# Attention with a gated state: work moved off VectorE, and the order of roots, sigmoid and projections

## The chip, the cores and the metric

The kernel runs on one core of a Trainium2 chip. It is one program in one launch. The time is the device time in microseconds of that core. A core has TensorE (PE, matrix products into PSUM), VectorE (DVE), ScalarE (ACT), GpSimd (POOL), and SyncE (SP), whose queue issues the transfers here. The engines run side by side, each through its own list of instructions in order, and meet only at semaphores.

## The reference, cut to what matters

The program computes four layers over 4096 tokens of width 256 (4 sequences of 1024): gated linear attention, a mixture of experts, a memory layer with one gradient step, and a ternary MLP, each followed by a layer norm. Only the first layer and its norm matter here:

```
q, k, v = x @ Wq.T, x @ Wk.T, x @ Wv.T            # 16 heads of 16
q, k = elu(q / 4) + 1, elu(k) + 1
gate = sigmoid(x @ Wg.T + bg)                     # one number per head and token
for t in range(1024):
    S = gate[t] * S + outer(k[t], v[t])           # 16 x 16 per head
    y[t] = q[t] @ S
x = layernorm(x + y @ Wo.T)
```

## The kernel before, in words

`build_attention` cuts each sequence into chunks of 128 tokens. A tile is one chunk of one sequence: 32 tiles j, with T = j // 4 the chunk and b = j % 4 the sequence, so that a block of four tiles shares the chunk. The last four tiles carry no state on (KEPT = 28).

Within a tile the recurrence becomes matrix products. DVE makes the decay matrix of all 16 heads by one scan over 2048 columns (`decay`, L515, tile a_dcy) from gates that SP has spread over 128 partitions (a_gbc). `weigh` (L524) multiplies the scores (L311) by it into a_A, in two instructions. `attend` (L323, L330) sums what the state gives (St times qE) and what the tile's own tokens give (A times v). Sums of decays (ET, L504, one scan for four tiles) are spread over heads by a matmul (`decays`, L271); `decayed_q` (L541) makes qE from it, and L544 copies the decay over the whole tile to a_dec. The state is renewed by `update`: PE multiplies k and v (L343, 16 records per tile); DVE masks the product to the heads' own blocks (a_um, L556) and adds the old state times a_dec, in two instructions (L560). In the first four tiles a masked copy does (L554). `residual` (L568) adds x to the output projection (L285), and bn_stats and bn_aggr (L572, L576) take its mean and variance. POOL computes the inverse root from these for four tiles at once (`spread`, three Newton steps in four operations each), ACT normalises (L450), PE turns the result (`turn_x`, L294), ACT keeps it (L441), PE scores it for the experts (`router`, L300) and ACT copies the scores (L445).

q and k are projected by `project` (L237), one of four quarters of a chunk in each turn. ACT makes elu from it in three activations (L406, L407, L409), POOL adds them into a_qk (`phi`, L610). The gates are projected once per chunk (L246); ACT takes their sigmoid (L416), whose table has to be loaded, and loads the table of exp again (L417). SP writes the gates out (L182) and reads them back spread (`gates_in`, L189), two tiles ahead.

The order is written out by hand: each engine runs a loop over n from FIRST to LAST - 1, and turn n does on each engine the steps of its tiles: scores of n + 1, output of n - 1, attend of n, projection of quarter n + 5, values and transposed k of n + 1, and the later steps of tiles n - 5 to n - 7. DVE in turn n: weigh n, update n - 1, weigh_k n (L532, a_kw), scan n + 1, decayed_q n + 1, residual n - 1, and, each fourth turn, the scan of ET.

Of the kernel before, what the change touches and what calls it, by code (L numbers as in the profile page):

```python
# [17 lines left out]
P = 128  # L18
# [54 lines left out]
def build_attention(nc, io, mem):  # L73

    X, XT, ident = mem["X"], mem["XT"], mem["ident"]
    with ExitStack() as c2:
# [35 lines left out]
        stat = sb("stat", [P, 6])  # L112
        mv = mem["mv"]
        nmean = sb("nmean", [P, B])
# [19 lines left out]
        y_ready, yt_done, u_ready, um_done, st_done = (sem(k) for k in ("y_ready", "yt_done", "u_ready", "um_done", "st_done"))  # L134
# [3 lines left out]
        n_done = sem("n_done")  # L138
        id_done = sem("id_done")
        FIRST, LAST, SP_OPS = -5, NT + 3, 15  # L140
# [13 lines left out]
        def state_read(e, j):  # L154

            if j < 4:
                e.wait_ge(st_done, 2 * (j + 1))
            else:
                e.wait_ge(um_done, j - 3)

        with nc.Block() as block:
            @block.sync
            def _(sp):
# [12 lines left out]
                sp.dma_start(blk[:, :, :], io["blk"]).then_inc(cst_in, 16)  # L176
                sp.dma_start(Wv[:, :, :], io["WvT"].rearrange("(g p) n -> p g n", p=P)).then_inc(wv_in, 16)
# [46 lines left out]
            def _(pe):  # L224
# [25 lines left out]
                def values(j):  # L250
# [5 lines left out]
                    if j >= 8:  # L256
                        pe.wait_ge(xnt_read, j - 7)
# [30 lines left out]
                def turn_x(j):  # L288
                    pe.wait_ge(xn_done, j + 1)
                    pe.wait_ge(v_read, 3 * min(j + 7, NT))  # L290
# [24 lines left out]
                def attend(j):  # L315

                    b = j % 4
                    if j >= 4:
                        pe.wait_ge(qe_done, j - 3)
                        pe.wait_ge(st_done, 2 * (j - 3))  # L320
# [13 lines left out]
                def update(j):  # L334
# [5 lines left out]
                    for g in range(G):  # L340
                        for r in range(4):
                            c = g * P + 32 * r
                            mm = pe.matmul(bK[32 * r:32 * r + 32, 32 * g:32 * g + 32], kw[j % 2][:, c:c + 32], vp[j % 2][:, c:c + 32],  # L343
                                           start=True, stop=True)
                    mm.then_inc(u_ready, 1)

                def turn_k(j):
                    T, b = divmod(j, 4)
                    pe.wait_ge(phi_done, 4 * (T + 1))
                    if j == 0:  # L350
                        pe.wait_ge(cst_in, 64)
# [11 lines left out]
                for n in range(FIRST, LAST):  # L363
# [5 lines left out]
                    if tile(n - 1):  # L369
                        project_out(n - 1)  # L370

                    if n >= -4:
                        if tile(n - 1):
                            pe.wait_ge(yt_done, n)
                        if 1 <= (n + 4) // 4 <= NC and n % 4 == 0:
                            pe.wait_ge(sig_done, (n + 4) // 4)
                        if carries(n - 8):
                            pe.wait_ge(r_read, n - 7)
                    if Q % 4 == 0 and Q < NT:
                        gates(Q // 4)  # L380
                    if carries(n - 7):
                        router(n - 7)
# [3 lines left out]
                    if Q < NT:  # L386
# [3 lines left out]
                    if carries(n - 6):  # L390
                        turn_x(n - 6)
# [6 lines left out]
            def _(act):  # L398
# [20 lines left out]
                def values(j):  # L419
                    act.wait_ge(v_ready, j + 1)  # L420
                    if tile(j - 7):
                        act.wait_ge(xnt_ready, j - 6)
# [15 lines left out]

                def keep_x(j):
# [3 lines left out]
                def score(j):  # L443
                    act.wait_ge(r_ready, j + 1)
                    act.activation(mem["score"][:, j, :], bY[:, R0:R0 + E8], ACT.Copy).then_inc(r_read, 1)  # L445

# [16 lines left out]
                for n in range(FIRST, LAST):  # L463
                    Q = n + 5
                    if n == -2:
                        act.wait_ge(cst_in, 64)
                    if tile(n + 2):
                        masked_q(n + 2)

                    if tile(n):  # L470
                        act.wait_ge(y_ready, n + 1)
                    elif carries(n - 7):
                        act.wait_ge(r_ready, n - 6)
                    if Q % 4 == 0 and Q < NT:
                        gates(Q // 4)
                    if carries(n - 7):
                        score(n - 7)
                    if tile(n):
                        y_out(n)
                    if Q < NT:  # L480
# [3 lines left out]
                    if carries(n - 6):  # L484
                        keep_x(n - 6)
                    if carries(n - 5):
                        normalize(n - 5)

            @block.vector
            def _(v):  # L490
# [8 lines left out]
                def gate_decay(T):  # L499
# [6 lines left out]
                    v.memset(gT[T % 2][:, 0:1], 0.0).then_inc(gz_done, 1)  # L506

# [27 lines left out]
                def decayed_q(j):  # L535
# [7 lines left out]
                    v.wait_ge(st_done, 2 * min(j - 1, KEPT))  # L543
                    v.tensor_copy(dec[j % 2][:, :], bK[:, HALF + P - 1:HALF + D:P]).then_inc(dec_done, 1)  # L544

                def update(j):
# [4 lines left out]
                    if j >= 1:  # L551
                        v.wait_ge(st_done, 2 * j)
                    if j < 4:
# [1620 lines left out]
```

## Time and profile before

| | us |
|---|---|
| three timed runs | 1461.71, 1460.06, 1454.76; median 1460.06 |
| the profiled execution | 1467.62 |
| its span | 1465.6 |
| attention, from the start to the barrier behind it | about 326 |
| one block of four tiles in its middle | 38.52 |

The span is one profiled execution. The attention stage fills its first 326 us; the stages behind it are the same instructions in both kernels, but for one of POOL. Busy time is a sum over instructions of one engine; neighbouring instructions overlap slightly, so that distances between starts are safer than durations. In a list of groups the columns are: line, engine, operation, output and inputs with their shapes, count, then busy us and mean ns of one, then the idle time before them and who ended it. In a timeline the columns are: start, us, engine, line, operation, shapes, count, and in brackets the idle time before it with its releaser.

### The profile page before, as it was taken

What the parts mean: (1) busy time and instruction counts of PE and PEld (TensorE: products, weight loads), DVE (VectorE), ACT (ScalarE), POOL (GpSimd) and SP (SyncE); (2) the same over time, 40 slices, a digit from 0 to 9 for tenths busy, and PEclk for the clock granted to TensorE, in tenths of its full rate; (3) what the DMA queues carried; (4) which work ended last, traced back from release to release, by engine and by line L of the source; (5) the groups of instructions that cost most, each with busy time, mean ns of one, the idle gap of its engine ahead of it and who ended that gap; (6) DMA issues with size and microseconds to landing.
All of it is one profiled execution on the core that took longest, in us unless ns stands there. A gap on an engine that the chain in (4) does not pass through costs nothing. (4 is left out here: it accounts for less than half of the span.)

```text
span 1465.6 us, 21869 instructions
## 1 busy us (share of the span) xinstructions
PE 1345.6 (92%) x7418; PEld 859.6 (59%) x7419; DVE 828.9 (57%) x1676; ACT 536.7 (37%) x1104; POOL 305.6 (21%) x357
## 2 busy tenths in 40 slices
PE   7888888889989899999999997869999999899996
PEld 4556656655545566666666664436665564477774
DVE  5999999986533222222222221457778755676774
ACT  5445554432011122222222221134444532457675
POOL 2133333321653000000000001613220000144444
PEclk9899999999999999999999999989999999999999
DMA  5544544629221011111111112303110000000001
GB/s 192 177 171 172 177 170 158 207 80 370 84 79 61 22 51 43 43 47 46 43 43 50 43 43 90 87 21 105 30 29 1 1 1 11 1 1 15 29 15 58
DMA packets 68226, 112.39 MB, mean 77 GB/s; under 512 B 9008, under 2 KB 53936, under 8 KB 64048
## 3 DMA queue, kind: packets, MB, share of 16 engines
q1 hardware_dynamic: 61584, 94.49, 19.2%
q0 software_dynamic: 6144, 16.79, 3.6%
q8 instruction: 50, 0.82, 0.2%
q14 instruction: 32, 0.26, 0.1%
q10 hardware_dynamic: 416, 0.03, 0.0%
HBM read 79.70 MB, written 31.59 MB: 76 GB/s over the span
## 5 line engine op out<-in xcount | busy, mean ns | idle before, releaser
L1684 POOL DMA_INDIRECT m_got<-outs,slot x64 | 61.2, 957 | 562.7 <-DMA outs<-XT 448.1
L1089 DVE TENSOR_TENSOR ro_h<-ro_bB,ro_sl 128x512 f32<-128x512 f32 x71 | 49.1, 692 | 218.5 <-PE ro_bB L1038 218.5
L515 DVE TENSOR_TENSOR_SCAN a_dcy<-a_gbc,a_ident 128x2048 f32<-128x2048 f32 x32 | 144.6, 4520 | 11.2 <-DMA a_gbc<-gd 7.3
L2040 POOL TENSOR_TENSOR q_hr<-q_hf,q_hr 128x512 fp32r<-128x512 f32 x64 | 83.9, 1322 | 287.0 <-ACT q_hr L1881 287.0
L1033 PE MATMUL ro_bA<-Win,ro_xT 128*128 x284 | 135.9, 601 | 0.7 <-ACT ro_xT L1060 0.6
L1045 PE MATMUL ro_bO<-Wout,ro_hT 128*128 x568 | 134.3, 379 | 0.9 <-DVE ro_hT L1082 0.9
L1045 PEld LDWEIGHTS ro_bO<-Wout,ro_hT 128*128 128x128 f32 x568 | 107.8, 190 | 45.6 <-issue 34.6
L1038 PE MATMUL ro_bB<-Wsw,ro_xT 128*128 x284 | 133.5, 592 | 0.0
L1082 DVE COPY ro_hT<-ro_bH 128x512 f32<-128x512 f32 x71 | 49.1, 691 | 101.2 <-PE ro_bH L1018 101.2
L1069 ACT ACTIVATE XT<-ro_bO 128x256 f32<-128x256 f32 x71 | 27.2, 383 | 204.9 <-PE ro_bO L1045 204.9
L1038 PEld LDWEIGHTS ro_bB<-Wsw,ro_xT 128*128 128x128 f32 x284 | 54.0, 190 | 68.2 <-issue 68.2
L1806 PE MATMUL q_bO<-W2r,q_hr 128*128 128x256 f32 x512 | 75.9, 294 | 6.8 <-POOL q_hr L2040 6.7
L610 POOL TENSOR_TENSOR a_qk<-a_eb,a_rb 128x512 f32<-128x512 f32 x32 | 40.6, 1269 | 182.7 <-ACT a_eb L409 182.2
L1064 ACT ACTIVATE ro_sl<-ro_bA 128x512 f32<-128x512 f32 x71 | 42.4, 597 | 97.3 <-PE ro_bA L1033 97.3
L1806 PEld LDWEIGHTS q_bO<-W2r,q_hr 128*128 128x128 f32 x512 | 66.1, 188 | 19.9 <-POOL q_hr L2040 14.2
L934 POOL DMA_INDIRECT rows<-r_row,r_rix x64 | 63.9, 999 | 65.5 <-DVE r_rix L835 47.9
L311 PE MATMUL a_bS<-a_qm,a_qk 32*128 32x256 f32 x512 | 39.3, 422 | 40.1 <-DVE a_A L524 28.4
L524 DVE TENSOR_TENSOR a_A<-a_bS,a_dcy 128x1024 f32<-128x1024 f32 x64 | 75.3, 1219 | 0.1
L1796 PE MATMUL q_bH<-q_xr,W1r 128*128 128x512 f32 x256 | 70.6, 404 | 3.6 <-ACT q_hr L1881 3.6
L1114 PE MATMUL m_ring<-m_h,m_W 128*128 128x512 f32 x128 | 60.0, 613 | 12.4 <-ACT m_alr L1405 8.9
L1033 PEld LDWEIGHTS ro_bA<-Win,ro_xT 128*128 128x128 f32 x284 | 48.8, 192 | 36.0 <-issue 35.7
L786 ACT ACTIVATE sh_sl<-sh_bA 128x512 f32<-128x512 f32 x28 | 16.6, 597 | 120.2 <-PE sh_bA L724 74.9
(271 smaller groups left out, 2524.1 us busy)
## 6 DMA issues: line engine op xcount, KB each, us to landing
a_gbc<-gd SPq DMA_DIRECT2D x32, 1024.0 KB, 4.8
rows<-a_zero SPq DMA_DIRECT2D x8, 1152.0 KB, 10.5
XT<-rows SPq DMA_DIRECT2D x71, 128.0 KB, 2.0
outs<-XT SPq DMA_DIRECT2D x71, 128.0 KB, 1.7
a_xt<-in_xTt SPq DMA_DIRECT2D x8, 512.0 KB, 3.7
X<-in_x SPq DMA_DIRECT2D x8, 512.0 KB, 5.8
Win<-in_w_in SPq DMA_DIRECT2D x8, 512.0 KB, 10.7
Wsw<-in_w_sw SPq DMA_DIRECT2D x8, 512.0 KB, 10.6
```

Source lines behind the costliest of these rows:

```text
L515: v.tensor_tensor_scan(dcy[:, :], gbc[j % 2][:, :], ident16[:, :], 0.0, ALU.mult, ALU.add).then_inc(d_done, 1)
L524: v.tensor_tensor(A[j % 2][:, 2 * h:2 * h + 2, :, :, :].rearrange("p r g e t -> p r g (e t)"), bS[:, 2 * h:2 * h + 2, :].rearrange("p r (g ...
L934: pool.indirect_dma_start(out=mem["rows"], out_offset=bass.IndirectOffsetOnAxis(ap=rix[p][k][:, 0:1], axis=0), in_=row[p][k][:, :], in_off ...
L1033: mm = pe.matmul(bA[:, :], xT[p][:, g, :], w, start=(g == 0), stop=(g == G - 1))
L1038: mm = pe.matmul(bB[:, :], xT[p][:, g, :], w, start=(g == 0), stop=(g == G - 1))
L1045: mm = pe.matmul(bO[:, 0:D], hT[:, j * P:(j + 1) * P], Wout[:, bass.ds(e, 1), j, :].rearrange("p o f -> p (o f)"), start=(j == 0), stop=(j ...
L1082: v.tensor_copy(hT[:, :], bH[:, :]).then_inc(ht_read, 1)
L1114: mm = pe.matmul(banks[o][:, :], W[:, i, col + o * P:col + (o + 1) * P], rhs(i), start=(i == 0), stop=(i == G - 1))
L1684: pool.indirect_dma_start(out=got[q % 2][k][:, t, :], out_offset=None, in_=mem["outs"], in_offset=bass.IndirectOffsetOnAxis(ap=slot[:, k, ...
L1796: mm = pe.matmul(bH[f % 2][:, :], W1r[:, g, f * P:(f + 1) * P], xr[q % 2][:, part, g, :], start=(g == 0 and part == 0), stop=(g == G - 1 a ...
L1806: mm = pe.matmul(bO[k // 2][:, (k % 2) * D:(k % 2 + 1) * D], hr[:, part, f % 4, k * P:(k + 1) * P], W2r[:, f, :], start=(f == 0 and part = ...
L2040: pool.tensor_tensor(hr[:, 1, f % 4, :], hf[f % 2][:, :], hr[:, 0, f % 4, :], ALU.subtract).then_inc(hl_done, 1)
```

## The change

- State: the DVE additions of L560 go. ACT makes from a_dec a 32 x 32 diagonal matrix per row group and half (`decay_matrix`, two activations of 32 columns), PE adds that matrix times the old state to the same PSUM columns as the product of k and v (16 more records), and DVE does one masked copy for every tile.
- Norm: bn_stats and bn_aggr go from DVE. ACT sums x and its squares about the mean in two activations with an accumulator (`moments`). POOL's root takes one operation less.
- The first four additions of q and k move from POOL to DVE.
- Order: `project` comes before router and attend on PE, and before y_out on ACT, in three turns of four. ACT takes the sigmoid of the gates at the end of the turn, behind project and values, instead of ahead of y_out. DVE takes the scan of ET right behind `weigh` of the next turn. Normalising, turning and scoring come two turns later, and so the loops are two turns longer (LAST = NT + 5).

```diff
-        um = sb("um", [P, G, 32])
+        eye32, dg = sb("eye32", [P, 32]), [sb(f"dg{p}", [P, G, 32]) for p in range(2)]
-        FIRST, LAST, SP_OPS = -5, NT + 3, 15
+        FIRST, LAST, SP_OPS = -5, NT + 5, 14
...
                 # PE, update(j)
-                                           start=True, stop=True)
+                                           start=(g == 0), stop=(j < 4), skip_group_check=True)
+                    if j >= 4:
+                        pe.wait_ge(dg_done, 2 * (j - 3))
+                        pe.wait_ge(st_done, j - 3)
+                        for g in range(G):
+                            for r in range(4):
+                                mm = pe.matmul(bK[32 * r:32 * r + 32, 32 * g:32 * g + 32], dg[j % 2][32 * r:32 * r + 32, g, :],
+                                               St[32 * r:32 * r + 32, j % 4, g, :], start=False, stop=True, skip_group_check=True)
...
                 # PE, the loop
                     if tile(n - 1):
                         project_out(n - 1)
+                    if Q < NT and Q % 4 > 0:
+                        project(Q)
                     if n >= -4:
                         if tile(n - 1):
                             pe.wait_ge(yt_done, n)
-                        if 1 <= (n + 4) // 4 <= NC and n % 4 == 0:
-                            pe.wait_ge(sig_done, (n + 4) // 4)
+                        if n % 4 == 0:
+                            pe.wait_ge(sig_done, min((n + 4) // 4 + 1, NC))
...
-                    if Q < NT:
+                    if Q < NT and Q % 4 == 0:
                         project(Q)
-                    if carries(n - 6):
-                        turn_x(n - 6)
+                    if carries(n - 8):
+                        turn_x(n - 8)
...
                 # ACT
+                def decay_matrix(j):
+                    act.wait_ge(dec_done, j - 3)
+                    if j >= 6:
+                        act.wait_ge(u_ready, j - 1)
+                    for g in range(G):
+                        act.activation(dg[j % 2][:, g, :], eye32[:, :], ACT.Copy, scale=dec[j % 2][:, g:g + 1]).then_inc(dg_done, 1)
+                def moments(j):
...
+                    act.activation(scrap[:, :], X[:, j, :], ACT.Copy, scale=-1.0 / D, accum_out=mv[T % 2][:, b, 0:1]).then_inc(bn_done, 1)
+                    act.wait_ge(bn_done, j + 1)
+                    act.activation(scrap[:, :], X[:, j, :], ACT.Square, bias=mv[T % 2][:, b, 0:1], accum_out=mv[T % 2][:, b, 1:2]).then_inc(ag_done, 1)
...
-                    if Q % 4 == 0 and Q < NT:
-                        gates(Q // 4)
...
                     if tile(n + 1):
                         values(n + 1)
+                    if 0 < Q < NT and Q % 4 == 0:
+                        gates(Q // 4)
+                    if carries(n - 8):
+                        keep_x(n - 8)
+                    if tile(n - 2):
+                        moments(n - 2)
+                    if carries(n - 7):
+                        normalize(n - 7)
...
                 # DVE, update(j)
-                    v.tensor_tensor(um[:, :, :], bK[:, 0:64].rearrange("p (g c) -> p g c", g=G), blk[:, :, :], ALU.mult).then_inc(um_done, 1)
-                    for g in range(G):
-                        v.scalar_tensor_tensor(out=St[:, b, g, :], in0=St[:, b, g, :], scalar=dec[j % 2][:, g:g + 1], in1=um[:, g, :],
-                                               op0=ALU.mult, op1=ALU.add).then_inc(st_done, 1)
+                    v.tensor_tensor(St[:, b, :, :], bK[:, 0:64].rearrange("p (g c) -> p g c", g=G), blk[:, :, :], ALU.mult).then_inc(st_done, 1)
...
                 # DVE, residual(j) and the loop
-                    v.bn_stats(stat[:, :], X[:, j, :]).then_inc(bn_done, 1)
-                    v.bn_aggr(mv[T % 2][:, b, :], stat[:, :]).then_inc(ag_done, 1)
                     if tile(n):
                         weigh(n)
+                    if n >= 0 and n % 4 == 0 and n // 4 + 1 < NC:
+                        gate_decay(n // 4 + 1)
                     if carries(n - 1):
                         update(n - 1)
...
-                    if Q % 4 == 0 and Q < NT:
-                        gate_decay(Q // 4)
+                    if n == FIRST:
+                        gate_decay(0)
+                    if Q < 4:
+                        phi(Q)
```

## Rows read from the trace of the kernel before

**Rows 1.** Busy time by stretches: from:to, us, then each engine (x count), clock, DMA.

```profile
150.00:200.00 50.00, 43.13 (x553) 30.29 (x554) 48.57 (x68) 25.60 (x69) 21.67 (x38) 1.00 0.49 168
```

**Rows 2.** The groups of DVE in the first 330 us.

```profile
L560 DVE SCALAR_TENSOR_TENSOR a_St<-a_St,a_dec,a_um 128x32 f32<-128x32 f32 x48 | 16.9, 392 | 0.8
L572 DVE BATCH_NORM_STATS2 a_stat<-X 128x6 f32<-128x256 f32 x32 | 13.7, 427 | 1.1
...
L576 DVE BATCH_NORM_AGGREGATE mv<-a_stat 128x2 f32<-128x6 f32 x32 | 5.8, 182 | 1.1
```

**Rows 3.** The timeline of DVE over one turn of the middle.

```profile
148.22 2.35 DVE L524 TENSOR_TENSOR a_A<-a_bS,a_dcy 128x1024 f32<-128x1024 f32 x2
150.50 0.21 DVE L556 TENSOR_TENSOR a_um<-a_bK,a_blk 128x64 f32<-128x64 f32 x1
150.75 0.41 DVE L560 SCALAR_TENSOR_TENSOR a_St<-a_St,a_dec,a_um 128x32 f32<-128x32 f32 x2
151.08 0.42 DVE L532 TENSOR_TENSOR a_kw<-a_bK,a_dcy 128x256 f32<-128x256 f32 x1
151.63 4.43 DVE L515 TENSOR_TENSOR_SCAN a_dcy<-a_gbc,a_ident 128x2048 f32<-128x2048 f32 x1
155.97 0.40 DVE L541 TENSOR_TENSOR a_qE<-a_bK,a_qk 128x256 f32<-128x256 f32 x1
...
156.35 0.42 DVE L568 TENSOR_TENSOR X<-a_bK,X 128x256 f32<-128x256 f32 x1
...
157.37 2.35 DVE L524 TENSOR_TENSOR a_A<-a_bS,a_dcy 128x1024 f32<-128x1024 f32 x2
...
159.89 1.07 DVE L560 SCALAR_TENSOR_TENSOR a_St<-a_St,a_dec,a_um 128x32 f32<-128x32 f32 x2
```

**Rows 4.** The timeline of DVE in the first four tiles.

```profile
53.68 0.21 DVE L554 TENSOR_TENSOR a_St<-a_bK,a_blk 128x64 f32<-128x64 f32 x1
53.81 0.41 DVE L532 TENSOR_TENSOR a_kw<-a_bK,a_dcy 128x256 f32<-128x256 f32 x1
```

**Rows 5.** The timeline of PE over a block of four tiles.

```profile
131.31 1.15 PE L311 MATMUL a_bS<-a_qm,a_qk 32*128 32x256 f32 x16 [1.33 <-POOL a_qk L610]
...
136.61 1.98 PE L237 MATMUL a_bQ<-a_xt,a_Wqk 128*128 128x512 f32 x4
...
139.87 0.44 PE L357 MATMUL a_bK<-ident,a_qk 128*128 128x128 f32 x2
...
150.72 1.15 PE L311 MATMUL a_bS<-a_qm,a_qk 32*128 32x256 f32 x16 [1.18 <-DVE a_A L524]
...
158.23 0.33 PE L343 MATMUL a_bK<-a_vp,a_kw 128*32 128x32 f32 x16
158.49 0.44 PE L357 MATMUL a_bK<-ident,a_qk 128*128 128x128 f32 x2
...
169.83 1.15 PE L311 MATMUL a_bS<-a_qm,a_qk 32*128 32x256 f32 x16 [1.33 <-POOL a_qk L610]
```

**Rows 6.** The timeline of ACT: gates, then a projection with its values.

```profile
60.02 1.28 ACT L416 ACT_TABLE_LOAD   x1 [7.07 <-issue]
61.32 0.37 ACT L416 ACTIVATE a_gT<-a_bY,a_bg 128x128 f32<-128x128 f32 x1
...
147.88 0.60 ACT L406 ACTIVATE a_nb<-a_bQ 128x512 f32<-128x512 f32 x1 [1.43 <-PE a_bQ L237]
...
149.68 0.41 ACT L429 ACTIVATE a_vp<-a_bV 128x256 f32<-128x256 f32 x1
```

**Rows 7.** The timeline of PE in the empty turns behind the last tile.

```profile
323.39 0.58 PE L300 MATMUL a_bY<-a_Wr,XT 128*128 128x8 f32 x4 [0.56 <-ACT XT L441]
...
324.81 0.58 PE L300 MATMUL a_bY<-a_Wr,XT 128*128 128x8 f32 x4 [0.56 <-ACT XT L441]
```

**Rows 8.** DMA issues: tensor, queue, count, KB each, us to landing.

```profile
a_gbc<-gd SPq DMA_DIRECT2D x32, 1024.0 KB, 4.8
rows<-a_zero SPq DMA_DIRECT2D x8, 1152.0 KB, 10.5
```

More of the change, by code:

```diff
@@ L420, in values @@
                     act.wait_ge(v_ready, j + 1)
-                    if tile(j - 7):
-                        act.wait_ge(xnt_ready, j - 6)
+                    if tile(j - 9):
+                        act.wait_ge(xnt_ready, j - 8)
                     if j >= 2:
@@ L465, in _ @@
                     if n == -2:
-                        act.wait_ge(cst_in, 64)
+                        act.wait_ge(cst_in, 80)
                     if tile(n + 2):
                         masked_q(n + 2)
+                    if 4 <= n < KEPT:
+                        decay_matrix(n)
+                    if Q < NT and Q % 4 > 0:
+                        project(Q)
                     if tile(n):
                         act.wait_ge(y_ready, n + 1)
-                    elif carries(n - 7):
-                        act.wait_ge(r_ready, n - 6)
-                    if Q % 4 == 0 and Q < NT:
-                        gates(Q // 4)
-                    if carries(n - 7):
-                        score(n - 7)
+                    elif carries(n - 9):
+                        act.wait_ge(r_ready, n - 8)
+                    if n == FIRST:
+                        gates(0)
+                    if carries(n - 9):
+                        score(n - 9)
                     if tile(n):
                         y_out(n)
-                    if Q < NT:
+                    if Q < NT and Q % 4 == 0:
                         project(Q)
@@ L631, in spread @@
                         link(pool.tensor_tensor(y, na[:, :], y, ALU.mult))
-                    link(pool.tensor_scalar(nmean[:, :], mv[T % 2][:, :, 0], -1.0, 0.0, ALU.mult, ALU.add))
-                    pool.tensor_tensor(shift[T % 2][:, :], nmean[:, :], y, ALU.mult).then_inc(sh_done, 1)
+                    pool.tensor_tensor(shift[T % 2][:, :], mv[T % 2][:, :, 0], y, ALU.mult).then_inc(sh_done, 1)
                     pool.wait_ge(sh_done, T + 1)
-                for Q in range(NT):
+                pool.wait_ge(phi_done, 4)
+                for Q in range(4, NT):
                     phi(Q)
-                    if Q % 4 == 1 and Q >= 9:
-                        spread((Q - 9) // 4)
-                for T in range((NT - 1 - 9) // 4 + 1, NC - 1):
+                    if Q % 4 == 3 and Q >= 11:
+                        spread((Q - 11) // 4)
+                for T in range((NT - 1 - 11) // 4 + 1, NC - 1):
                     spread(T)
@@ L2161 @@
         "hmask": ((p[:, None] // 16) % 2 == np.arange(2)[None, :]).astype(np.float32),
+        "eye32": np.tile(np.eye(32, dtype=np.float32), (4, 1)),
         "blk": np.stack([(p[:, None] // 16) % 2 == np.arange(32)[None, :] // 16] * G, axis=1).astype(np.float32),
```

74 lines of the change are left out of this document (32 added, 42 removed).

## The prediction

> **What bounds the kernel now.** The change lies in the attention stage, from the start to about 326 us of the 1465.6 us span, so only that stage counts. I read the busy time by stretches first: between 150 and 200 us VectorE (DVE) is busy 48.57 of 50 us, TensorE (PE) 43.13, ScalarE (ACT) 25.60 [rows 1]. DVE is the bound, but PE is right behind it, and that is where this forecast gets its size. The list of DVE groups shows what the change takes from DVE: 48 state updates of L560 (16.9 us), 32 bn_stats of L572 (13.7 us), 32 bn_aggr of L576 (5.8 us) [rows 2], together 36.4 us. That is the ceiling, not the forecast.
>
> The timeline of DVE then gives one turn (one tile): two halves of a_A start at 148.22 and again at 157.37, so a turn is 9.15 us, with no gap [rows 3]. PE's timeline gives the same cadence from the other side: scores of L311 start at 131.31 and four turns later at 169.83, so a block of four turns (one of them with the gates of L246) is 38.52 us [rows 5].
>
> **DVE's own new turn.** Instructions overlap a little, so I take distances between starts. Residual (156.35) to the next a_A (157.37) is 1.02 us [rows 3]; without the two statistics the add alone is left, 0.42 us busy less some 0.09 of overlap, 0.33: 0.69 goes. a_um (150.50) to a_kw (151.08) is 0.58 [rows 3]; with a single masked copy it is 53.68 to 53.81, 0.13 [rows 4]: 0.45 goes. So 9.15 - 1.14 = 8.0 us. In about every second turn the pair of L560 takes 1.07 instead of 0.41 [rows 3]; that 0.66 goes with it.
>
> **PE's own turn.** In a turn without gates PE goes from scores at 150.72 to the transpose of k at 158.49, 7.77 us, and the transpose itself takes 0.44 by its record, less the overlap of neighbours of about 0.1 (158.23 to 158.49 is 0.26 for a record of 0.33): 8.1 us of pure order, which today hides behind 9.15. The change adds 16 matmul records (decay matrix times state). The 16 of the same kind at L343 take 0.26 from start to start (158.23 to 158.49) [rows 5]. Lower bound 0, if they overlapped wholly; upper bound 16 times the 0.07 us of a 256-column scores matmul (1.15 for 16), 1.1. I take 0.3, near L343, which has the same 32 columns. PE's turn is 8.4 us. The turn with gates is 139.87 - 131.31 = 8.56, plus 0.33 and 0.3: 9.2.
>
> **The two together.** After the k transpose starts, DVE does: 0.65 until a_St (its end and the signal; between 0.44, the transpose's own length, and 0.9), 0.13 to a_kw, 0.55 to the scan (151.08 to 151.63), 4.34 to qE, about 0.4 for qE and dec, 0.33 residual, 2.35 for a_A, 0.15 to the scores that wait for it (a_A from 148.22 lasts to 150.57, scores start at 150.72) [rows 3, 5]: 8.9. From those scores to the transpose PE needs 7.77 + 0.3 = 8.1. The loop spans two turns, 17.0 / 2 = 8.5 us. So the ordinary turn becomes 8.5: PE and DVE are level, and of DVE's saving of 1.14 plus half of 0.66 only about 1 us a turn arrives.
>
> **The order of gates.** On PE the projection of L237 goes ahead of attend in three turns of four; the same instructions, so PE's sum does not change, while POOL's add into qk comes 2 us earlier. That removes the 1.33 us wait of the scores at 131.31 for POOL [rows 5], which is inside the 38.52. ACT now does the gates' sigmoid after project and values of the same turn instead of before y_out, and DVE asks for it right after the a_A of the next tile, ahead of update, a_kw and the scan. Counted from the scores of the gate turn (t = 0): PE's projection starts at 136.61 - 131.31 = 5.30 and takes 1.98, so ACT's first activation comes at 7.3; from there to the end of vp is 149.68 + 0.41 - 147.88 = 2.2, so 9.55; table load 1.28, sigmoid 0.37 [rows 5, 6]: 11.2. DVE's a_A ended at 8.1. It stands still for 3.1 us, and behind it in its queue stand the scan of ET (0.5), the state copy, a_kw and the long scan. PE meanwhile runs its scores, then its decays wait for a_kw: 11.2 + 0.5 + 0.13 + 0.55 = 12.4 instead of 10.3 (9.2 and the 1.15 of the scores). a_A then ends at 11.2 + 0.5 + 0.2 + 0.5 + 4.34 + 0.7 + 2.35 = 19.8, with the signal and start gaps 20.0, and scores follow. The gate turn and its successor take 20.0 where free ones would take 9.2 + 8.5 = 17.7: 2.3 us of new wait per block. Block: 20.0 + 2 x 8.5 = 37.0 against 38.52, **1.5 us saved**, where without that wait it would be 3.8.
>
> The Trainium skill (ScalarE: Activation LUTs, "What ACT_TABLE_LOAD costs") puts a switch of tables at 1283 ns of load and about 1380 ns of drain. Here the load at 60.02 takes 1.28 and the sigmoid starts at 61.32, right at its end [rows 6], so the trace shows the load and no drain behind it; by the page's rule the stall would be 1.4 us longer in each of seven blocks, some 10 us more, and by the row it is as summed above.
>
> **ACT's other additions.** Two activations for the moments (nearest: the 0.41 of a vp of the same 128x256 [rows 6], so 0.8 for the pair and at most twice that; I take 1.1, since the second waits for the first) and two of 32 columns for the decay matrix (less than two vp, 0.8; I take 0.3). Its turn has 25.60 of 50 us busy [rows 1], 4.7 a turn, and becomes about 6.2 of 8.5: hidden in ordinary turns. After the gate turn it runs late, to t = 14.6, and the next projection on PE ends at 15.7, so it has caught up. If the moments cost 2 us each that cover would be gone in the gate turn only.
>
> **Start.** The four first adds of qk go from POOL to DVE, which is idle there; gain up to 1 us, loss up to 0.7. The first gates have the stall of 3.1 too, and three turns at about 1.1 give it back by tile 4: 0, between -2 and +3. **Blocks.** Tiles 4 to 7 have no router and no turn of x yet, so ACT's sigmoid comes 1 us sooner: -3.8. Tiles 8 to 11 partly so: -2.2. Tiles 12 to 27, four blocks: -6.0. **Tiles 28 to 31** have no projection and PE is short there, so DVE's saving arrives whole: 4 x 0.69, plus one state update, -3.1. **Tail.** Normalising, turning and scoring lag two turns more, so two more empty turns are run after the last tile. One takes 324.81 - 323.39 = 1.42 us [rows 7]: +2.8, and the moments of the last tiles fall into that chain: +1.1. Sum: 0 - 3.8 - 2.2 - 6.0 - 3.1 + 3.9 = **-11.2 us**. The later stages keep their instructions (one tiny POOL operation goes), 0.
>
> The profiled run took 1467.6 us, with a span of 1465.6 and 2 around it; by the sum it becomes 1456.4. The median of the timed runs is 1460.06, so I forecast 1460.1 - 11.2 = **1449 us**. What a measurement of this kernel tells from no change is about 0.5%, 7.3 us; the forecast is 0.77%.
>
> **Rivals.**
> A. No gate stall: ACT reaches the sigmoid in time, or DVE's wait lies in slack. For it: ACT is idle half of the time. Against: the order of instructions puts three PE-dependent activations ahead. It would give 2.3 x 6 + about 3 at the start more: -28, 1432 us.
> B. DVE's whole saving arrives (8.0 a turn, PE not in the way, stall as forecast): 0.5 x 20 turns more, -21, 1439 us. Against it: 8.1 of pure PE order even without the new matmuls.
> C. The added matmuls or the accumulation into one place cost 0.7 to 1.1 rather than 0.3: turn 8.9 to 9.2; 24 turns x 0.4 = +10 at the nearer value: 1459 us, no change. For it: pairs that write the same PSUM columns, never seen in this order.
> D. Slower: the decays from HBM come late. On SP's queue the writing out of the gates waits for the memset behind ET and stands ahead of the load of a_gbc two tiles on. It could go at t = 11.7 + 1.7 = 13.5, lands 4.8 later [rows 8], 18.3, and the scan wants it at 20.6. It decides once landing takes over 7.1 us; at 10.5, as the row of the cleared rows has, each of seven blocks loses 3.4: +24 - 11, 1473 us. Against it: all 32 landings have a median of 4.8.
> E. The gate stall is longer: the hand-over between two kinds of function on ACT costs once more what the load shows, 1.28 in each of seven blocks, +9: 1458 us. For it: DVE, PE and SP all wait on that one sigmoid; against it: at 61.32 it follows at once.
>
> **Chances.** Forecast 0.45, A 0.15, B 0.12, C 0.13, D 0.06, E 0.09. The forecast's own spread is 1443 to 1455. Faster by over 0.5% (under 1452.8): most of the forecast (0.33) and A and B, 0.60. Within 0.5%: the rest of the forecast, C and E less a part that overshoots, 0.30. Slower: D and the far end of C, 0.10. Range 1432 to 1462.
>
> **What would show it.** Scores of L311 8.4 to 8.6 us apart in ordinary turns; one DVE wait of about 3 us a block before ET, released by ACT's sigmoid, and a PE gap of about 2 us before the decays; the new dg matmuls adding 0.3; ACT's moments near 1.1 a turn; a tail 4 us longer; the end of attention near 315 us instead of 326. Wrong if turns are under 8.1 or over 8.9, if DVE does not wait for the sigmoid, or if it waits for a_gbc.

## The result, and the profile after

The changed kernel takes 1455.34 us (median of 20 runs, 1452.65 to 1458.90), the kernel before 1459.63 (20 runs, 1454.01 to 1463.14): ratio 0.9978, interval 0.9967 to 0.9988. By the ratio that is 3.2 us less (1.8 to 4.8); the two medians lie 4.3 apart. 11.2 less were forecast: the sign is right, the time lies in the range, the size is about a third. The profiled execution took 1453.86 us, with a span of 1452.1.

The busy time of the middle stretch of the kernel after, in the order of [rows 1] (PE, PEld, DVE, ACT, POOL, clock, DMA):

```profile
150.00:200.00 50.00, 47.43 (x680) 33.67 (x679) 43.10 (x45) 35.50 (x107) 13.69 (x21) 1.00 0.49 166
```

DVE fell from 48.57 to 43.10, PE rose from 43.13 to 47.43. The heavier load is now PE's, which the forecast put level with DVE; yet neither is full, so something stops both.

The starts of scores give the stage its clock marks. First the kernel before on PE (tiles 4, 8, 28, 31, then the first product of the next stage), then the kernel after at the same places:

```profile
53.91 0.81 PE L311 MATMUL a_bS<-a_qm,a_qk 32*128 32x256 f32 x4 [2.26 <-DVE a_A L524]
...
92.79 0.50 PE L311 MATMUL a_bS<-a_qm,a_qk 32*128 32x256 f32 x4 [1.38 <-POOL a_qk L610]
...
285.36 0.93 PE L311 MATMUL a_bS<-a_qm,a_qk 32*128 32x256 f32 x12 [1.33 <-POOL a_qk L610]
...
311.12 1.15 PE L311 MATMUL a_bS<-a_qm,a_qk 32*128 32x256 f32 x16 [2.32 <-DVE a_A L524]
...
325.98 1.44 PE L724 MATMUL sh_bA<-XT,Ws 128*128 128x512 f32 x2 [0.59 <-PEq L161]
```

```profile
55.80 0.93 PE L308 MATMUL a_bS<-a_qm,a_qk 32*128 32x256 f32 x12 [1.39 <-DVE a_A L560]
...
91.81 1.15 PE L308 MATMUL a_bS<-a_qm,a_qk 32*128 32x256 f32 x16
...
280.65 1.15 PE L308 MATMUL a_bS<-a_qm,a_qk 32*128 32x256 f32 x16
...
304.15 1.15 PE L308 MATMUL a_bS<-a_qm,a_qk 32*128 32x256 f32 x16 [1.63 <-DVE a_A L560]
...
325.54 2.05 PE L747 MATMUL sh_bA<-XT,Ws 128*128 128x512 f32 x2 [0.58 <-PEq L157]
```

Differences of these starts, with tile 12 at 131.31 [rows 5] and at 129.40 (below):

| stretch | forecast | measured |
|---|---|---|
| start to tile 4 | 0 | +1.9 |
| tiles 4 to 8 | -3.8 | -2.9 |
| tiles 8 to 12 | -2.2 | -0.9 |
| tiles 12 to 28, four blocks | -6.0 | -2.8 (+0.2, -1.4, -0.2, -1.4) |
| tiles 28 to 31 (forecast for four turns, measured over the three between these starts) | -3.1 | -2.3 |
| tail, scores of 31 to the next stage | +3.9 | +6.5 |
| sum | -11.2 | -0.4 |

In this pair of executions attention is only 0.4 us shorter; the ratio of the timed runs gives 3.2. The spans of the two executions differ by 13.5 us, nearly all of it behind attention, where the instructions are the same but for one: 4.4 us in the stage right behind it, 1.5 in the next, and 7.1 in the memory layer, where PE waits once for ACT's m_alr (L1405 before), 8.9 us in the one execution and 1.7 in the other. That execution of before was 8 us above its median.

**The place of the gates.** The waits between 60 and 300 us in the kernel after (engine, what waits, releaser: us in total, times, longest):

```profile
DVE a_ET L536 <- ACT a_gT L422: 18.4, 6, 3.5
...
PE a_bK L268 <- DVE a_kw L568: 12.8, 6, 2.3
```

So once a block DVE stands 3.1 us for ACT's sigmoid, and PE 2.1 us for DVE. The timelines around one such wait, DVE, then ACT:

```profile
135.31 2.35 DVE L560 TENSOR_TENSOR a_A<-a_bS,a_dcy 128x1024 f32<-128x1024 f32 x2
141.16 0.42 DVE L536 TENSOR_TENSOR_SCAN a_ET<-a_gT,a_zeros 128x128 f32<-128x128 f32 x1 [3.50 <-ACT a_gT L422]
...
142.38 4.42 DVE L551 TENSOR_TENSOR_SCAN a_dcy<-a_gbc,a_ident 128x2048 f32<-128x2048 f32 x1
```

```profile
137.24 0.60 ACT L412 ACTIVATE a_nb<-a_bQ 128x512 f32<-128x512 f32 x1 [1.43 <-PE a_bQ L234]
...
139.04 0.41 ACT L435 ACTIVATE a_vp<-a_bV 128x256 f32<-128x256 f32 x1
139.46 1.28 ACT L422 ACT_TABLE_LOAD   x1
140.76 0.37 ACT L422 ACTIVATE a_gT<-a_bY,a_bg 128x128 f32<-128x128 f32 x1
```

The sigmoid is last in a chain that starts with PE's projection: elu, values, table load, sigmoid, the order that was forecast. DVE's ET is at its queue's head and holds the state, a_kw and the long scan behind it. The sigmoid starts 0.02 us after its table load ends, as in [rows 6].

PE around the same wait, two turns. It starts with a turn that carries gates:

```profile
128.77 0.33 PE L347 MATMUL a_bK<-a_St,a_dg 32*32 32x32 f32 x16
129.03 0.44 PE L361 MATMUL a_bK<-ident,a_qk 128*128 128x128 f32 x2
129.40 1.15 PE L308 MATMUL a_bS<-a_qm,a_qk 32*128 32x256 f32 x16
...
132.49 0.67 PE L243 MATMUL a_bY<-a_xt,a_WgT 128*32 128x128 f32 x16 [0.44 <-DMA a_xt<-in_xTt]
...
139.10 1.15 PE L308 MATMUL a_bS<-a_qm,a_qk 32*128 32x256 f32 x16
142.35 1.01 PE L268 MATMUL a_bK<-a_ET,a_rep 128*128 128x128 f32 x4 [2.11 <-DVE a_kw L568]
143.16 1.92 PE L282 MATMUL a_bK<-a_Wo,a_yT 128*128 128x256 f32 x4
144.86 2.43 PE L234 MATMUL a_bQ<-a_xt,a_Wqk 128*128 128x512 f32 x4
147.13 0.51 PE L297 MATMUL a_bY<-a_Wr,XT 128*128 128x8 f32 x4
...
151.32 1.15 PE L308 MATMUL a_bS<-a_qm,a_qk 32*128 32x256 f32 x16
...
159.72 1.15 PE L308 MATMUL a_bS<-a_qm,a_qk 32*128 32x256 f32 x16
```

And the same wait three blocks later:

```profile
253.03 1.15 PE L308 MATMUL a_bS<-a_qm,a_qk 32*128 32x256 f32 x16
256.28 0.68 PE L268 MATMUL a_bK<-a_ET,a_rep 128*128 128x128 f32 x4 [2.11 <-DVE a_kw L568]
256.80 1.03 PE L282 MATMUL a_bK<-a_Wo,a_yT 128*128 128x256 f32 x4
...
259.38 0.51 PE L297 MATMUL a_bY<-a_Wr,XT 128*128 128x8 f32 x4
...
263.86 1.15 PE L308 MATMUL a_bS<-a_qm,a_qk 32*128 32x256 f32 x16 [0.22 <-DVE a_A L560]
```

The wait is 2.11 both times, but behind the first the output projection takes 1.92 instead of 1.03. From decays to router PE needs 4.78 us there and 3.10 here, and the turn is 12.22 instead of 10.83. The granted clock (the share of full speed that the chip allowed TensorE) is the difference (140 to 150 and 254 to 264 us, PE alone: us, busy, clock, DMA):

```profile
140.00:150.00 10.00, 7.89 (x76) 0.83 0.54 199
254.00:264.00 10.00, 7.67 (x112) 1.00 0.53 195
```

A mean of 0.83 is a stretch at 1.2 GHz within one at 2.4. The turns behind the gates are 11.6, 12.12, 12.22, 10.83, 12.03 and 10.83 us (from the scores of tiles 5, 9, 13, 17, 21 and 25 to the next), and the mean clock of the 12 or 13 us around each is 0.86, 0.87, 0.87, 1.00, 0.87 and 1.00: the clock falls in four of six. The Trainium skill (TensorE: Matmul & The Clock Gate, Part 1) says of the clock's rise under a stream of matrix products that its place varies from run to run. This trace shows something related and not the same: within one execution the same wait is followed by a fall or by none.

The first such wait, at the start of the stage, is longer: DVE stands 5.35 us, PE 5.24, and the scores behind it take 2.09 us instead of 1.15. DVE, then PE:

```profile
31.03 0.42 DVE L536 TENSOR_TENSOR_SCAN a_ET<-a_gT,a_zeros 128x128 f32<-128x128 f32 x1 [5.35 <-ACT a_gT L422]
```

```profile
39.09 2.09 PE L308 MATMUL a_bS<-a_qm,a_qk 32*128 32x256 f32 x16 [5.24 <-DVE a_A L560]
```

**The tail.** PE in the last empty turns, to be held against [rows 7]:

```profile
316.76 0.58 PE L297 MATMUL a_bY<-a_Wr,XT 128*128 128x8 f32 x4 [0.56 <-ACT XT L454]
318.19 0.44 PE L291 MATMUL a_bV<-ident,X 128*128 128x128 f32 x2 [0.84 <-ACT X L474]
319.19 0.58 PE L297 MATMUL a_bY<-a_Wr,XT 128*128 128x8 f32 x4 [0.56 <-ACT XT L454]
...
321.88 1.00 PE L297 MATMUL a_bY<-a_Wr,XT 128*128 128x8 f32 x4 [0.56 <-ACT XT L454]
```

An empty turn takes 2.43 and 2.69 us instead of 1.42: the transpose now waits for ACT's normalising (L474), which stands behind ACT's moments. Then PE's clock falls too (0.50 from 320 to 326 us; router 1.00 instead of 0.58), and the next stage begins with a product of 2.05 for 1.44.

**ACT's additions**, groups of the first 330 us:

```profile
L469 ACT ACTIVATE a_scrap<-X,mv 128x256 f32<-128x256 f32 x32 | 16.3, 508 | 1.0
L467 ACT ACTIVATE a_scrap<-X 128x256 f32<-128x256 f32 x32 | 13.7, 427 | 0.0
L450 ACT ACTIVATE a_dg<-a_eye,a_dec 128x32 f32<-128x32 f32 x48 | 12.4, 306 | 0.0
...
L467 ACT ACTIVATION_READ_ACCUMULATOR a_scrap<-X 128x1 f32 x32 | 6.8, 213 | 0.0
```

### The profile page after: what moved, and what is told of

It is laid out like the page before. It is cut to its first block and busy times, and to the rows that moved or that the text cites. A ratio compares the mean times of both kernels' runs of the same rounds, so it can differ in the third digit from the quotient of the medians.

```text
span 1452.1 us, 22698 instructions
## 1 busy us (share of the span) xinstructions
PE 1355.7 (93%) x7802; PEld 867.7 (60%) x7803; DVE 795.5 (55%) x1568; ACT 582.2 (40%) x1280; POOL 299.8 (21%) x345
## 3 DMA queue, kind: packets, MB, share of 16 engines
q1 hardware_dynamic: 61728, 94.51, 19.5%
## 5 line engine op out<-in xcount | busy, mean ns | idle before, releaser
L551 DVE TENSOR_TENSOR_SCAN a_dcy<-a_gbc,a_ident 128x2048 f32<-128x2048 f32 x32 | 141.6, 4425 | 4.1 <-DMA a_gbc<-gd 0.2
L633 POOL TENSOR_TENSOR a_qk<-a_eb,a_rb 128x512 f32<-128x512 f32 x28 | 37.1, 1324 | 190.5 <-ACT a_eb L415 190.5
L560 DVE TENSOR_TENSOR a_A<-a_bS,a_dcy 128x1024 f32<-128x1024 f32 x64 | 75.1, 1216 | 0.1
L1902 ACT ACTIVATE q_hf<-q_bH,q_b 128x512 f32<-128x512 f32 x64 | 44.2, 690 | 37.6 <-PE q_bH L1818 36.4
```

What stands on the lines that cost most here:

```text
L551: v.tensor_tensor_scan(dcy[:, :], gbc[j % 2][:, :], ident16[:, :], 0.0, ALU.mult, ALU.add).then_inc(d_done, 1)
L560: v.tensor_tensor(A[j % 2][:, 2 * h:2 * h + 2, :, :, :].rearrange("p r g e t -> p r g (e t)"), bS[:, 2 * h:2 * h + 2, :].rearrange("p r (g ...
```

## The experiments

Each kernel is the changed one with the edit shown, unless the text says otherwise. "Last scores" is the start of the scores of tile 31 (304.15 after), "next stage" the first product behind attention (325.54 after). Each ratio is to the kernel before on the same chip; where kernels ran on different chips, the starts in their traces are compared and not their times.

**Gates back in their place.** ACT's sigmoid ahead of y_out, DVE's ET at the end of the turn, as in the kernel before.

```diff
 # ACT, turn n
-                    if n == FIRST:
-                        gates(0)
+                    if Q % 4 == 0 and Q < NT:
+                        gates(Q // 4)
...
-                    if 0 < Q < NT and Q % 4 == 0:
-                        gates(Q // 4)
 # DVE, turn n: behind weigh(n), then at the end
-                    if n >= 0 and n % 4 == 0 and n // 4 + 1 < NC:
-                        gate_decay(n // 4 + 1)
...
-                    if n == FIRST:
-                        gate_decay(0)
+                    if Q % 4 == 0 and Q < NT:
+                        gate_decay(Q // 4)
```

> The changed kernel with one part undone: ACT's sigmoid ahead of y_out and DVE's scan of ET at the end of the same turn, as in the kernel before; lighter DVE steps, early projection and the lag of two turns stay. Theory S (the gate wait took the gain): the DVE wait of 2.2 to 3.5 us before ET goes, PE's 2.1 us gap before the decays goes, and with it the stretches at the lower clock behind it; the pair of turns at a gate falls from 20.3 to 21.9 us to 9.4 + 8.4 = 17.8; scores of the last tile start near 283 us instead of 304, time near 1436 us. Rival P (PE is the bound anyway, the gate wait only shows slack): last scores start after 300 us and the time stays within 3 us of 1455. Rival Y (a late y_out takes its place): DVE's wait goes but PE waits for ACT's yT or for values in the gate turn; last scores near 295, time near 1447.

Measured: 1435.61, ratio 0.9847 (0.9823 to 0.9871), as theory S has it; rivals P and Y are false. Last scores at 284.12, 20.0 earlier: 3.9 of that by tile 3 (43.88 for 47.79), the rest in six blocks, one of which takes 35.16 us (155.38 to 190.54; after 38.72). The turn with gates and the next take 9.59 + 8.77:

```profile
155.38 1.15 PE L308 MATMUL a_bS<-a_qm,a_qk 32*128 32x256 f32 x16
...
164.97 1.15 PE L308 MATMUL a_bS<-a_qm,a_qk 32*128 32x256 f32 x16
...
173.74 1.15 PE L308 MATMUL a_bS<-a_qm,a_qk 32*128 32x256 f32 x16 [0.31 <-DVE a_A L558]
```

The same stretch of all engines as in [rows 1]:

```profile
150.00:200.00 50.00, 49.02 (x728) 34.43 (x726) 46.47 (x50) 36.48 (x104) 20.43 (x35) 1.00 0.56 187
```

PE is busy 49.02 of 50, and the clock is 1.00 in each of the five stretches of 50 us from 50 to 300. In ACT's timeline the sigmoid now waits only for PE's attend, and DVE waits for it 1.4 us in three blocks in all, where it was 18.4 in six:

```profile
123.97 1.28 ACT L422 ACT_TABLE_LOAD   x1 [1.42 <-issue]
126.05 0.37 ACT L422 ACTIVATE a_gT<-a_bY,a_bg 128x128 f32<-128x128 f32 x1 [0.80 <-PE a_bY L327]
```

At the last scores the rest of the change brings 27.0 us (311.12 to 284.12); the gates' new place takes 20.0 of them back.

**Only DVE's ET late.** ACT as changed, DVE's ET behind the long scan at the end of the turn n = 4m; SP's writing out of the gates follows the load of a_gbc.

```diff
 # DVE, turn n
                     weigh(n)
-                    if n >= 0 and n % 4 == 0 and n // 4 + 1 < NC:
-                        gate_decay(n // 4 + 1)
...
                     residual(n - 1)
+                    if n >= 0 and n % 4 == 0 and n // 4 + 1 < NC:
+                        gate_decay(n // 4 + 1)
```

> The changed kernel with ACT's order left as it is; only DVE takes the scan of ET at the end of its turn behind the residual instead of right behind a_A, and SP loads a_gbc two tiles on before it writes the gates out. Theory S: the same gain as undoing the whole order, last scores near 283 us, time near 1436, since the sigmoid comes at 11.2 us of the gate turn and is asked for at 17. Rival P: last scores after 300 us, no gain. Rival G (the transfers of the gates come late, since they are written 5 us later): DVE waits for a_gbc at the scan of the fourth tile of each block, 2 to 4 us; time near 1450.

Measured: 1439.71, ratio 0.9865 (0.9839 to 0.9891). Last scores 287.71, where 283 was expected: 3.6 later than with the gates back, 2.9 of it by tile 3 (46.73 for 43.88); the pair behind the gates 9.5 + 9.11. So the wait is where DVE asks, not that ACT is late: with the sigmoid at the same late place it is gone from 60 us on when DVE asks after the scan. No wait for a_gbc appears, although the gates are written out later here (rival G), and in the changed kernel itself the only one is 0.2 us, at the start, which makes rival D false. The tail is 23.25 instead of 21.39: in the turn of tile 31 PE's clock falls (output projection 1.92 for 1.03; 0.55 from 289 to 292 us).

**Normalising ahead of the moments**, in ACT's turn.

```diff
-                    if tile(n - 2):
-                        moments(n - 2)
...                  # behind normalize
+                    if tile(n - 2):
+                        moments(n - 2)
```

> The changed kernel with normalize ahead of moments on ACT, nothing else. Theory T (the tail's length is the chain turn x, keep, moments, normalise): each of the three tail turns with moments gets 1.2 us shorter, from the last scores to the next stage 21.4 us become 18 to 19, last scores stay at 304 us; time 2 to 3 us lower, near 1452. Rival: the tail is set by PE at its lower clock and by the number of turns, then it gets less than 0.7 us shorter.

Measured: 1453.52, ratio 0.9969 (0.9956 to 0.9982), so 4.5 us less than before, 1.3 more than the change alone; the two intervals overlap. The trace shows it better: last scores 303.07, next stage 322.56, 19.5 later instead of 21.4, a little less than expected. An empty turn is 1.85 us (router 315.20 to 317.05), not the 1.42 of before: the transpose goes at once, but ACT's copy of it waits behind the moments (1.00 instead of 0.56 on PE).

**Both edits together**, the two diffs above.

> Both edits: scan of ET at the end of DVE's turn (with the load of a_gbc ahead of the writing out), and normalize ahead of moments. If the gate wait and the tail are separate losses their gains add: last scores near 283 us, 18 to 19 us from there to the next stage, time near 1433. If the tail only fills time that the next stage would wait for anyway, it is the time of the first edit alone, 1436.

Measured: 1437.63, ratio 0.9853 (0.9827 to 0.9879); last scores 288.26, next stage 307.75, 17.8 us before that of the changed kernel, where the two edits alone bring 14.6 and 3.0. So they add up in the trace; in the times the second is 2.1 us, within the intervals.

**Parts undone, with the gates in their old place.** This kernel, the next two and the kernel before with the late gates ran on another, slower chip (before: 1469.61 there), so ratios and traces count. The state's addition back on DVE:

```diff
-                    if j >= 4:      # PE, update(j)
-                        ... 16 matmuls dg x St
+                    for g in range(G):      # DVE, update(j)
+                        v.scalar_tensor_tensor(out=St[:, b, g, :], in0=St[:, b, g, :], scalar=dec[j % 2][:, g:g + 1], in1=um[:, g, :], ...)
```

> The changed kernel with the gates in their old place and, beside that, the state update back on DVE (masked copy and two additions of the old state; no decay matrix on ACT, no added products on PE). Theory L (turn = mean of two chains: 8.9 us from the transpose of k to the next but one scores, 7.8 on to the transpose, and PE's own order): DVE's chain grows by 0.45 and PE's shrinks by 0.26, so the ordinary turn stays at 8.4 to 8.6 us, last scores near 286 us against 284 with the decay matrix, time near 1438: moving the state update bought almost nothing. Rival D (DVE's steps arrive one for one): turn 8.85, last scores near 295, time near 1446. Rival B (PE is the sole bound): turn 8.1, last scores near 279, time near 1430.

Measured: ratio 0.9869 (0.9816 to 0.9923); ordinary turns 8.45 to 8.54, gate pair 9.02 + 9.79; last scores 288.38, so the diagonal matrix is worth 4.3 us. The turn is that of theory L, the gain twice its 2 us; rivals D (295) and B (279) are false.

bn_stats and bn_aggr back on DVE, moments gone from ACT, and POOL's root with its one operation again:

```diff
-                        moments(n - 2)      # ACT
+                    v.bn_stats(stat[:, :], X[:, j, :]).then_inc(bn_done, 1)      # DVE, residual(j)
+                    v.bn_aggr(mv[T % 2][:, b, :], stat[:, :]).then_inc(ag_done, 1)
```

> The changed kernel with the gates in their old place and, beside that, mean and variance back on DVE (bn_stats and bn_aggr), none on ACT; lag and number of turns stay. Theory L: DVE's turn is 8.0 + 0.69 = 8.7 and the loop over two turns gives 8.8, so the ordinary turn grows by 0.4 us, the last four by 0.7; the tail loses the moments from its chain (3 us). Last scores near 295 us, next stage 18 us later, time near 1443. Rival: if ACT's longer turn were the hidden bound, taking 1.2 us a turn from it would keep the turn at 8.4 and the time would fall below 1433.

Measured: ratio 0.9891 (0.9836 to 0.9946); turns 8.69 to 8.81, 8.19 in the last; last scores 296.19, next stage 314.15, a tail of 18.0, as theory L has it. So the moments are worth 12.1 us up to the last scores, and they cost 3.4 behind them (21.39 for 17.96).

Normalising ahead of the moments and the gates back, their two diffs together:

> The changed kernel with the gates in their old place and normalize ahead of moments on ACT. Both gains should add: last scores near 284 us, next stage 19 us later instead of 21.4, time near 1433.5, the fastest so far. If the tail's gain is only in how late PE's clock comes back, it is 1435.6 as without the second edit.

Measured: ratio 0.9840 (0.9789 to 0.9890), last scores 284.25, next stage 303.74, as expected. The same kernel beside those of the last three experiments, on their chip:

> The kernel with the gates in their old place and normalize ahead of moments, with two buffers of xt, once more, beside the one with three: ratio to before 0.983 to 0.985 as at the first time, last scores at 284 us. It is there as the base of the other three on the same chip.

Measured: 1434.25, ratio 0.9836 (0.9820 to 0.9853), 284.13 and 303.62: the trace repeats to 0.12 us.

**The kernel before with the late gates alone.** None of DVE's work is taken away here; the diff is against the kernel before. PE's wait for the sigmoid ahead of attend is moved with it, as in the change.

```diff
 # ACT, turn n: ahead of y_out, then at the end
-                    if Q % 4 == 0 and Q < NT:
-                        gates(Q // 4)
+                    if n == FIRST:
+                        gates(0)
...
+                    if 0 < Q < NT and Q % 4 == 0:
+                        gates(Q // 4)
 # DVE, turn n: behind weigh(n)
+                    if n >= 0 and n % 4 == 0 and n // 4 + 1 < NC:
+                        gate_decay(n // 4 + 1)
```

> The kernel before with one thing of the change alone: ACT's sigmoid at the end of its turn and DVE's scan of ET right behind the next a_A. Theory S (the place of the sigmoid costs by itself): the sigmoid comes at about 11 us of the gate turn, DVE asks at 9, and since DVE is the bound every microsecond of its wait is lost: 2 us in each of six blocks and 3 at the start, and perhaps PE's clock with it; time 1470 to 1478 against 1459. Rival (the wait hurts only where the turn is short): no wait over 0.5 us, time within 3 us of 1459.

Measured: 1501.35, ratio 1.0221 (1.0158 to 1.0285), 32 us more, where 11 to 19 were expected; in the trace the next stage starts 29.6 later (355.59 for 325.98). Its DVE, then its PE, around one gate:

```profile
104.54 2.36 DVE L526 TENSOR_TENSOR a_A<-a_bS,a_dcy 128x1024 f32<-128x1024 f32 x2
109.52 0.42 DVE L506 TENSOR_TENSOR_SCAN a_ET<-a_gT,a_zeros 128x128 f32<-128x128 f32 x1 [2.62 <-ACT a_gT L416]
...
121.58 0.23 DVE L558 TENSOR_TENSOR a_um<-a_bK,a_blk 128x64 f32<-128x64 f32 x1 [2.25 <-PE a_bK L343]
```

```profile
111.19 0.68 PE L271 MATMUL a_bK<-a_ET,a_rep 128*128 128x128 f32 x4 [2.85 <-DVE a_kw L534]
...
115.00 1.94 PE L330 MATMUL a_bY<-a_A,a_vz 128*32 128x128 f32 x32
```

The first wait is what was priced. The fall behind it had only a "perhaps" and no price: PE's clock halves (0.50 from 112 to 116 us; attend 1.94 for 1.08), so that PE is late for DVE in its turn, 2.25 us. The turn behind the gates takes 12.1 to 15.3 us, where the same turn of the kernel before takes 9.6 to 9.9.

**Order alone.** The diffs of the gates, of the state and of the moments (with POOL's one operation) together: gates back, and both of DVE's savings undone. What is left is the early projection, the first four additions on DVE and the later roots.

> The changed kernel with the gates in their old place and all of DVE's steps back on DVE (state update and both statistics): what is left of the change is the early projection, the first adds on DVE and the lag of two turns. By the chains of one turn DVE is the sole bound again at 9.15 us, but POOL's add no longer meets the state update (0.66 in every second turn) and no scores wait for it: a block of four takes 37.1 instead of 38.5 us, last scores near 301 us against 311 before; the two more turns cost 2.8 of it. Time about 7 us under the kernel before. Rival (the order alone gives nothing, all of the 23 us come from the lighter steps): blocks of 38.5, last scores near 311, time 2 to 3 us above before because of the tail.

Measured: 1454.02, ratio 0.9975 (0.9961 to 0.9990). A block is 37.8 us (9.69, 9.78, 9.15, 9.15) for 38.52, last scores 305.84 where 301 was expected: 5.3 us from the order, but 4.7 go again in the tail (19.6 for 14.9). Of these 3.1 are the two more turns (the run with bn_stats and bn_aggr back has the same order there and a tail of 18.0), and 1.6 are the clock, which falls here in the turn of tile 31 (0.50 from 307 to 310 us; output projection 1.91 for 1.03).

**All projections after attend.** Gates back, `project` where it was.

```diff
-                    if Q < NT and Q % 4 > 0:
-                        project(Q)
...                  # behind attend (PE), y_out (ACT)
-                    if Q < NT and Q % 4 == 0:
+                    if Q < NT:
                         project(Q)
```

> The changed kernel with the gates in their old place and every projection behind attend on PE and behind y_out on ACT, as in the kernel before; lighter DVE steps stay. If the early projection matters, POOL's add of qk falls at the start of the next turn and holds DVE's scan up by 0.7 to 1.2 us in three turns of four, and the scores at a block's end wait for a_qk again: turns of 8.8 to 9.1 instead of 8.4, last scores near 294 us against 284, time 9 us above that kernel. Rival (order on PE is free while PE's sum is the same): last scores within 2 us of 284.

Measured: 1441.68, ratio 0.9889 (0.9873 to 0.9906). Last scores 289.59, where 294 was expected: the early projection is worth 5.5 us. POOL's a_qk is late once a block again, 6.6 us in 6, but only the turn ahead of that wait is longer (9.5 for 8.4), and not each, as expected.

**A third buffer for x.** The gates' product waits for the load of x (0.98 us at worst with the gates back); a third buffer lets that load start a chunk earlier. Gates back, normalising first.

```diff
-        xt = [sb(f"xt{p}", [P, G, B * P]) for p in range(2)]
+        xt = [sb(f"xt{p}", [P, G, B * P]) for p in range(3)]
...
-                    if n % 4 == 2 and n // 4 + 2 < NC:
-                        load_x(n // 4 + 2)
+                    if n % 4 == 2 and n // 4 + 3 < NC:
+                        load_x(n // 4 + 3)
```

> The gates in their old place, normalize ahead of moments, and a third buffer for xt, loaded a chunk earlier, so that PE's gates need not wait for a load that starts when the last values of the block are read. Expected: the waits of the gates for xt (0.2 to 1.0 us in each of six blocks, 2.0 in all between 60 and 300 us) go, last scores near 282 us instead of 284.2, time 2 us under the same kernel with two buffers. Rival: the wait hides in DVE's turn and scores do not come earlier; or the additional load at the start delays the first a_gbc, then the start is 1 us later.

Measured: 1431.90, ratio 0.9822 (0.9805 to 0.9840), last scores 281.44, next stage 301.09, as expected. It is the fastest of all, 2.4 us under its twin on the same chip and 25.5 under the kernel before.

## Why the forecast was right in kind and wrong in size

- **The ordinary turn** was forecast at 8.5 us and is 8.40. That is PE's own order as summed, 8.4; the loop through both engines, which gave the 8.5, does not bind. In these turns DVE waits for PE's transpose (9.6 us in 15 waits from 60 to 300 us), and with the gates back PE is busy 49.0 of 50. The 16 new products add 0.26 (128.77 to 129.03; forecast 0.3). The moments took 1.0 us a tile (142.81 to 143.85; 1.1), the diagonal matrix 0.52 (0.3). Rivals B (turn 8.0) and C (8.9) are false.
- **The gate wait** was placed and timed right: 3.1 for DVE, 2.1 for PE, pair 20.0; where the clock held it is 9.50 + 10.83 = 20.3. Rivals A, D and E are false: the wait exists, a_gbc is never late, and no second hand-over cost shows.
- **The step that failed** is the price of that wait: "20.0 where free ones would take 17.7: 2.3 us of new wait per block". The sum takes PE at its full clock throughout and so puts at nothing what follows the wait: PE's 2.1 us of standing still are followed by a stretch at 1.2 GHz in four of six blocks. From tile 12 on two blocks show it bare. Where the clock held they save 1.4 us each, of the 1.5 forecast; where it fell they save -0.2 and 0.2, and their turns behind the gates are 12.22 and 12.03 for 10.83. These 2.6 us are most of the miss of 3.2 in the four blocks. Against the same pairs with the gates back, the late gates cost 2.0 where the clock held and 2.5 to 3.2 where it fell, 15.8 us in six blocks; with 3.9 at the start and 0.3 elsewhere they are the 20.0 us at the last scores.
- Two smaller readings of that step were off. The free pair is 18.4 and not 17.7 (9.59 + 8.77), and 0.4 of that is the load of x, which was not looked at: the gates' product comes earlier than it (0.44 at 132.49, 1.3 us in five waits), and with a third buffer the gate turn is 9.18, the 9.2 of the forecast.
- **The first blocks.** For tiles 4 to 7 the reason given, a sigmoid 1 us sooner, takes 1.0 off a wait of 2.3; the forecast took off all of it (-3.8). It measured -2.9, with a fall of the clock inside it (turn 11.62, clock 0.86), and tiles 8 to 11 -0.9 for -2.2, again with a fall.
- **The start** was put at 0: a stall of 3.1, given back by three lighter turns. It is +1.9. With the gates back tile 4 starts 2.0 earlier than in the kernel before (51.89 for 53.91), so the stall costs 3.9: DVE stands 5.35 us for the sigmoid, and PE's scores of tile 2 run at half clock (2.09 for 1.15; 0.54 from 39 to 44 us).
- **The tail** was put at +3.9 and is +6.5. Two more turns were 2.8 and are 3.1 (18.0 for 14.9 with bn_stats and bn_aggr on DVE). The moments were put at 1.1 once and cost 3.4, since ACT does them ahead of the normalising in each empty turn, and PE's clock falls there too. Turning the two about gave 1.9 back.

What the parts are worth at the last scores, from the pairs above: gates' place -20.0 (lost), moments +12.1, early projection +5.5, order in all +5.3, diagonal matrix +4.3; the moments are worth 17.5 when DVE still has the state's addition (305.84 to 288.38), and the diagonal matrix 9.7 when DVE still has bn_stats and bn_aggr (305.84 to 296.19). So the parts do not add: each takes DVE nearer to PE's 8.4. These are worths up to the last scores, from one profile each; the tail comes on top.

**Open.** Attention is 0.4 us shorter in this pair of profiles, the ratio gives 3.2 and the medians 4.3. The order alone shows the same gap: 0.6 us in attention (325.43 for 325.98), 3.6 by its ratio. There is one profile of the kernel before, so it stays open whether its attention was shorter there than usual or the later stages gain a few us in the changed kernels.

That the gate wait brings the fall is well supported: in the kernel before and in the ten others without this wait the clock is 1.00 in all three stretches from 100 to 250 us. But the wait does not bring the fall each time. With the moments last and the gates late the same instructions hold it in four of six blocks (turns of 11.05 and 10.83 to 10.84), where the changed kernel holds it in two. Nor does it take a wait of 2 us: in three kernels it falls in the turn of tile 31 behind waits of 1.6 to 2.3 us, and in the changed kernel and the one before it does not, behind 1.63 and 2.32. What decides was not found, and how often the clock falls over many executions was not counted, so no share of the 8 us between 11.2 and 3.2 can be put to it with certainty.

## What to carry to other kernels

When work is taken off the bounding engine, look first at which engine is second and how near, and at what stands at the head of each queue: an instruction that waits for another engine belongs as late in its queue as its readers allow, or its producer as early, because all that is behind it waits too. A wait of 2 us on PE can cost more than 2 us: add the stretch at half clock that may follow, here 1.1 to 1.4 us. And of a change made of several parts, try each part's place alone: here one placement ate 20 us of 27.

## What the runs showed of the hardware that was not expected

- An activation with an accumulator is two instructions on ACT: 427 and 508 ns for 128x256, and ACTIVATION_READ_ACCUMULATOR of 186 to 213 ns behind it.
- A wait of 2.11 us on PE was followed by a stretch at 1.2 GHz in some blocks and not in others. Against the same turn with the clock held the fall cost 1.1 us (12.12 for 11.05) to 1.4 (12.22 for 10.83). In the kernel before with the late gates, where PE waits 2.85, wait and fall together lengthen the turn behind the gates by 2.3 to 5.4 us.
- Shorter waits can be followed by it too: behind 1.63 us before the scores of tile 31 the clock was 0.55 from 289 to 292 us in the run with only ET late, and 1.00 with the gates back, where the wait is 1.64.
